# All transposes of the activation on VectorE, in squares of 32x32, in place of TensorE

## The reference: what must be computed

```python
gate = lora_add(einsum('bnh,fh->bnf', x, W_gate), x, A_gate, B_gate)   # 512 -> 1376
up   = lora_add(einsum('bnh,fh->bnf', x, W_up),   x, A_up,   B_up)
act  = silu(gate) * up
down = lora_add(einsum('bnf,hf->bnh', act, W_down), act, A_down, B_down) # 1376 -> 512
return x + down
# lora_add(base, inp, A, B) = base + (inp @ A[i].T) @ B[i].T * 0.5, i by batch
```

## Time and profile before

| | us |
|---|---|
| median of 3 runs | 559.76 (559.27 to 559.87) |
| the profiled execution | 559.44 |
| its span | 557.6 |
| TensorE busy | 519.3 (93%) |
| VectorE busy | 260.4 (47%) |
| ScalarE busy | 199.9 (36%) |
| GpSimd busy | 39.8 (7%) |

### The profile page before, as it was taken

One profiled execution on the slowest core, in us unless ns is written; L12 is line 12 of the kernel. 1 busy time (PEld: TensorE's weight loads), 2 busy tenths in 40 slices (PEclk: granted clock), 3 DMA queues, 4 the chain that ended last, 5 costly groups with the idle time before them and its releaser, 6 DMA issues.

```text
span 557.6 us, 10117 instructions
## 1 busy us (share of the span) xinstructions
PE 519.3 (93%) x3169; PEld 472.5 (85%) x3169; DVE 260.4 (47%) x558; ACT 199.9 (36%) x427; POOL 39.8 (7%) x55
## 2 busy tenths in 40 slices
PE   0098899999999999999999999999999999999997
PEld 0097787989898989999898989898989898999986
DVE  7894266544444435353435353534444443435341
ACT  4890008333333433243323233323333343324221
POOL 1015700100000000000000000000000000000000
PEclk9999899999999999999999999999999999999999
DMA  7799991312030404030303031211203040403000
GB/s 288 293 303 389 325 322 44 78 47 78 22 105 6 118 0 117 6 111 13 111 13 106 18 92 32 83 41 52 71 22 101 7 116 0 120 3 111 13 21 19
DMA packets 32306, 53.19 MB, mean 95 GB/s; under 512 B 7586, under 2 KB 16194, under 8 KB 32290
## 3 DMA queue, kind: packets, MB, share of 16 engines
q1 hardware_dynamic: 32290, 53.00, 31.0%
HBM read 48.69 MB, written 4.28 MB: 95 GB/s over the span
## 4 chain that ended last, share of the span: by engine, by line
PE 86%; DVE 6%; DMA 4%; ACT 1%; issue 1%; SPq 0%; DVEq 0%
PE ps_g L962 21%; PE ps_u L962 20%; PE ps_db L1000 13%; PE ps_da L1000 13%; PE ps_x L991 3%; PE ps_x L942 3%; PE ps_g L916 2%; DMA toep<-kpad 2%; PE ps_u L916 2%; PE ps_g L972 2%; PE ps_u L972 2%; PE ps_g L973 2%; PE ps_u L973 2%; DMA kpad<-k_sb 2%; PE ps_x L1034 1%
## 5 line engine op out<-in xcount | busy, mean ns | idle before, releaser
L470 ACT CAST b_spl<-b_raw 64x512 fp32r<-64x512 f32 (+1 forms) x96 | 54.4, 569 | 98.6 <-PE ps_u L973 79.5
L780 DVE TENSOR_TENSOR b_spl<-b_raw,b_spl 64x512 fp32r<-64x512 f32 (+1 forms) x96 | 60.4, 630 | 53.7 <-ACT b_spl L470 50.1
L962 PE MATMUL ps_g<-w_hi,x_hi 128*128 128x512 f32 (+1 forms) x192 | 72.7, 379 | 1.4 <-DVE x_lo L874 1.4
L962 PE MATMUL ps_u<-w_hi,x_hi 128*128 128x512 f32 (+1 forms) x192 | 71.4, 372 | 0.0
L962 PE MATMUL ps_u<-w_lo,x_hi 128*128 128x512 f32 (+1 forms) x192 | 71.3, 371 | 0.0
L962 PE MATMUL ps_u<-w_hi,x_lo 128*128 128x512 f32 (+1 forms) x192 | 71.3, 371 | 0.0
L962 PE MATMUL ps_g<-w_lo,x_hi 128*128 128x512 f32 (+1 forms) x192 | 71.1, 370 | 0.0
L962 PE MATMUL ps_g<-w_hi,x_lo 128*128 128x512 f32 (+1 forms) x192 | 71.0, 370 | 0.0
L816 DVE TENSOR_TENSOR h_act<-h_act,ps_u 128x512 f32<-128x512 f32 (+1 forms) x48 | 30.3, 632 | 54.3 <-PE ps_u L973 54.2
L1000 PE MATMUL ps_da<-wd_hi,ht_hi 128*128 128x288 f32 (+1 forms) x176 | 54.6, 310 | 0.0
L1000 PE MATMUL ps_db<-wd_hi,ht_hi 128*128 128x288 f32 (+1 forms) x176 | 53.3, 303 | 0.0
(11 more groups left out here) (169 smaller groups left out, 894.4 us busy)
## 6 DMA issues: line engine op xcount, KB each, us to landing
a_raw<-atab SPq DMA_DIRECT2D x64, 152.0 KB, 2.4
toep<-kpad SPq DMA_DIRECT2D x16, 512.0 KB, 6.8
b_raw<-btab SPq DMA_DIRECT2D x128, 64.0 KB, 2.1
um<-xr SPq DMA_DIRECT2D x16, 256.0 KB, 4.7
x<-xT SPq DMA_DIRECT2D x8, 512.0 KB, 7.9
w_raw<-wgu SPq DMA_DIRECT2D x8, 512.0 KB, 9.1
out<-y_sb SPq DMA_DIRECT2D x15, 256.0 KB, 2.1
b_raw<-btab SPq DMA_DIRECT2D x64, 44.0 KB, 1.8
```

The source lines that it names most:

```text
L470: nc.scalar.copy(b_spl[0:LR, up, 0:w], b_raw[slot][:, up * w:(up + 1) * w]).then_inc(b_hi, 1)
L780: V.tensor_tensor(b_spl[LR:P, up, 0:w], b_raw[slot][:, up * w:(up + 1) * w], b_spl[0:LR, up, 0:w].bitcast(F32), ALU.subtract).then_inc(b_l ...
L962: T.matmul(ps[:, 0:w], xs[:, q, kb, :], ws[:, kb, col:col + w], start=(kb == 0 and xs is x_hi and ws is w_hi), stop=False)
```

## The change

The blocks of 128x128 on TensorE are gone. `transpose_act` is now a function of VectorE. It is called with a chunk and with the quarters of the tokens that it is to do (`froms`). One instruction takes 32 tokens (partitions `tok * 32` on of `h_act`) and, of each block of 128 columns, the 32 that begin at `to * 32`; it transposes the 4 (in the last chunk 3 or 2) squares of 32x32 and writes them to partitions `to * 32` on of the bank. 16 instructions make a chunk. The calls are put between VectorE's other work: chunks 0 and 1 in two halves, chunk 2 in one piece. With it `gated(2)`, `b_lo_part(na, nq, 0, .)` and, on ScalarE, `ht_hi_part(1)` move. The waits of the old function move along, save the wait for `amaskt_ok`, which is VectorE's own earlier work. The last block of chunk 2 has 96 hidden rows; its `to` = 3 has two squares.

```diff
--- before.py
+++ after.py
@@ -24,6 +24,7 @@
 NM = 64
 NF = 1376
 FB = -(-NF // P)
+Q = 32
 FLAST = NF - (FB - 1) * P
 R = 16
 BT = 4
@@ -531,10 +532,10 @@
                     top_part(NP_GU + 5)
                 ht_hi_part(0)
                 silu(2)
+                ht_hi_part(1)
                 if not last:
                     b_hi_part(na, nq, 0, 0)
                     b_hi_part(na, nq, 0, 1)
-                ht_hi_part(1)
                 act.wait_ge(res_ps, t + 1)
                 wait(act, y_out, 16 * t)
                 nc.scalar.copy(y_sb[:, :], ps_x[0][:, :]).then_inc(res_ok, 1)
@@ -815,6 +816,28 @@
                     dve.wait_ge(u_ps, n + 1)
                     V.tensor_tensor(h_act[:, s, 0:w], h_act[:, s, 0:w], ps_u[s][:, 0:w], ALU.mult).then_inc(act_ok, 1)
 
+                def transpose_act(c, froms):
+
+                    nf, w = BLK[c][1], CH[c][1]
+                    s = (NC * q + c) % 2
+                    bank = [0, 1, 1][c]
+                    if froms[0] == 0:
+                        dve.wait_ge(act_ok, NC * t + c + 1)
+                        if c == 0:
+                            dve.wait_ge(tm_ok, t + 1)
+                        elif c == 1:
+                            wait(dve, tdlo_ok, t)
+                        else:
+                            dve.wait_ge(htlo_ok, (NC + 1) * t + 2)
+                    for tok in froms:
+                        for to in range(P // Q):
+                            n = len(range(to * Q, w, P))
+                            flat = h_act[tok * Q:(tok + 1) * Q, s, :].rearrange("t (f q) -> t f q", q=P)
+                            into = ps_x[bank][to * Q:(to + 1) * Q, :].rearrange("q (f t) -> q f t", t=P)
+                            ins = V.transpose(into[:, 0:n, tok * Q:(tok + 1) * Q], flat[:, 0:n, to * Q:(to + 1) * Q])
+                    if froms[-1] == P // Q - 1:
+                        ins.then_inc(ht_ps, 1)
+
                 def ht_lo_part(c):
                     f0, nf = BLK[c]
                     bank = [0, 1, 1][c]
@@ -837,6 +860,7 @@
                 b_lo_part(a, q, 1, 0)
                 gated(0)
                 b_lo_part(a, q, 1, 1)
+                transpose_act(0, (0, 1))
                 if not first:
                     finish(t - 1)
                 dve.wait_ge(bd_hi, t + 1)
@@ -845,21 +869,24 @@
                 if first:
                     rem_part(NP_GU + 2)
                     rem_part(NP_GU + 3)
+                transpose_act(0, (2, 3))
                 b_lo_part(a, q, 2, 0)
                 gated(1)
                 b_lo_part(a, q, 2, 1)
+                transpose_act(1, (0, 1))
                 if first:
                     rem_part(NP_GU + 4)
                     rem_part(NP_GU + 5)
                 ht_lo_part(0)
+                transpose_act(1, (2, 3))
+                gated(2)
                 if not last:
                     b_lo_part(na, nq, 0, 0)
-                gated(2)
-                if not last:
-                    b_lo_part(na, nq, 0, 1)
                 ht_lo_part(1)
+                transpose_act(2, (0, 1, 2, 3))
                 if not last:
                     x_lo_part(na, nq, False)
+                    b_lo_part(na, nq, 0, 1)
                 ht_lo_part(2)
                 dve.wait_ge(ad_ps, t + 1)
                 wait(dve, td_ps, t)
@@ -973,25 +1000,6 @@
                     T.matmul(ps[:, 0:w], t_lo[:, up, :], b_spl[:, up, 0:w], start=False,
                              stop=True).then_inc(u_ps if up else g_ps, 1)
 
-                def transpose_act(c):
-                    f0, nf = BLK[c]
-                    s = (NC * q + c) % 2
-                    bank = [0, 1, 1][c]
-                    pe.wait_ge(act_ok, NC * t + c + 1)
-                    if c == 0:
-                        pe.wait_ge(tm_ok, t + 1)
-                    elif c == 1:
-                        wait(pe, tdlo_ok, t)
-                        if first:
-                            pe.wait_ge(amaskt_ok, 1)
-                    else:
-                        pe.wait_ge(htlo_ok, (NC + 1) * t + 2)
-                    for f in range(nf):
-                        rows = P if f0 + f < FB - 1 else FLAST
-                        ins = T.transpose(ps_x[bank][0:rows, f * P:(f + 1) * P], h_act[:, s, f * P:f * P + rows],
-                                          ident[:, :])
-                    ins.then_inc(ht_ps, 1)
-
                 def down(f, bank):
 
                     rows = P if f < FB - 1 else FLAST
@@ -1023,11 +1031,9 @@
                 for up in range(2):
                     base(1, up)
                     lora(1, up)
-                transpose_act(0)
                 for up in range(2):
                     base(2, up)
                     lora(2, up)
-                transpose_act(1)
 
                 pe.wait_ge(htlo_ok, (NC + 1) * t + 1)
                 for kb in range(KB):
@@ -1038,7 +1044,6 @@
                     pe.wait_ge(w_rem_dve, len(pieces) - NP_POOL)
                 pe.wait_ge(ad_lo, t + 1)
                 down_chunk(0)
-                transpose_act(2)
                 pe.wait_ge(htlo_ok, (NC + 1) * t + 2)
                 down_chunk(1)
                 if not last:
```

## The result

| | before | after |
|---|---|---|
| median of 4 runs, us | 559.76 | 669.22 (668.14 to 670.18) |
| ratio to before | | 1.195, 95% interval 1.193 to 1.198 |
| span of the profiled execution, us | 557.6 | 667.4 |
| VectorE / TensorE busy | 47% / 93% | 75% / 81% |
| one middle tile, us | 29.4 | 36.0 |

What follows compares the result with a forecast made beforehand. TensorE bounds the kernel before, VectorE's loop after: 12.1 (first tile) + 14 x 6.3 + 5.0 (last) = 105.3 us more, span 557.6 to 663, so 665 us; own range 635 to 700, overall 590 to 710.

Steps and rivals of the forecast that it cites:

- What bounds, and the turn-over: TensorE bounds before, 29.42 us per tile; after, the loop over VectorE does, 35.7 us, 6.3 more per tile.
- The transposes, 16.1 us per tile: On VectorE, 48 added transposes per tile: 32 at 0.35 us, 12 at 0.317 and 4 at 0.283.
- a square's filling: In each VectorE transpose, 32 columns' time added for filling one square: 0.03 us.
- Held apart: On VectorE, successive transposes write other partitions, so they start 0.32 us apart before filling, like `t_lo`, not 0.21.
- The loop without the squares, 9.43 + 10.2: Per tile, 9.43 us from last `down` blocks to next `gated(0)`, then 10.2 us of VectorE's old instructions and ScalarE detour.
- The waits: TensorE idles 7.5 us per tile: some 0.4 for `b_lo(2,0)`, then 2.2, 1.8 and 3.0 for the three `ht_lo`.
- First tile: Last `down` blocks start at 122.0 instead of 109.91, 12.1 us later; VectorE also splits weights there.
- The last tile: From `gated(0)` to the last blocks 24.3 us instead of 19.24, 5.0 us more.
- Rival 3: On TensorE, the granted clock falls in its new waits; chance 0.11.
- Rivals 1, 2 and 4: 1: overlap, 545 us, 0.03; 2: not held apart, 592 or 566, 0.12; 4: other rate, 759 or 619, 0.05/0.03.

Runs made afterwards that it cites:

- dose runs: The changed kernel with half or a quarter of the transposes left out, two PSUM fills added: 551.95 us (24 per tile) and 594.85 us (36 per tile).
- the exchanged loops: The changed kernel with the two inner loops, over `tok` and `to`, exchanged, so the output's place stays and the input's changes: 670.16 us.
- the filler run: The changed kernel with matmuls nobody reads put ahead of TensorE's waits for `ht_lo(1)` (4) and `ht_lo(2)` (9): 656.21 us, ratio 1.173.
- the copies: The changed kernel with a plain copy in place of each transpose, same places and sizes: 640.58 us, ratio 1.144.

## Why the prediction was right, and where it was not

- **What bounds, and the turn-over: right.** TensorE was the bound; the loop that runs over VectorE from `gated(0)` to `ht_lo(2)` became it. The dose runs show both sides of the knee.
- **The transposes, 16.1 us per tile: mis-sized by 0.7.** Measured 15.4. The spacing of 128 columns was 0.333 us, not 0.35: the gap after a held transpose is 0.01 us where I took the 0.04 of `t_lo`. The 0.03 us for a square's filling were my estimate, and no run shows a filling; what the runs show in its place is a transpose that lasts 33 ns longer than a copy of the same places.
- **Held apart: right, its reason too narrow.** I gave the output's place alone; the exchanged loops show that the input's counts as well. Had I relied on that reason to propose a better loop order, I would have been wrong by some 45 us.
- **The loop without the squares, 9.43 + 10.2: right.** 15.4 added gives 35.0; the filler run has 35.15.
- **The waits: right in place**, and each of the three for `ht_lo` 0.2 us shorter than forecast, once the idle-before is read as said above.
- **First tile: right but for the squares.** Its last `down` blocks start at 121.29, forecast 122.0; 11.4 us later than before, not 12.1. The last tile takes 23.65 us from `gated(0)` to its last blocks, 4.4 more than before, not 5.0.
- **Rival 3, the clock: it came, beside the forecast and not in its place.** I gave it 0.11, with a fall in every tile. The one fall of before has a mean clock of 0.66 over 5 us, and 0.50 in the stretch from 61 to 64 us; that makes, as an estimate, 3.4 us at half speed and up to 1.7 us lost per fall. In the kernel after a fall cost 1.5 us in every second tile: behind the first, behind 7 of the 14 middle ones and behind the last, 14 us in all.
- **That the number is within 4 us is luck.** At full clock the steps add up to 11.4 + 14 x (25.71 + 9.45 - 29.42) + 4.4 = 96 us, where I had 105: 9 us too much, nearly all of it the squares. The clock's 14 us were left out. 96 + 14 = 110 is what the span grew by (667.4 - 557.6), and two errors of opposite sign left 665 for a measured 669.
- **Rivals 1, 2 and 4: excluded** by the spacing of 0.333 us, and for the faster rate by the copies (0.92 ns a column).

## What to carry to other kernels

Work moved to an engine that is half idle fits only in the gaps that end before the next reader's deadline: follow the loop between the two engines step by step (here 9.4 + 10.2 us against TensorE's 28.2 left room for 8.6 us at most, and 24 transposes of 7.7 us, standing where they did, already cost 0.4), and move as much as fits there. Sixteen of the 48 transposes gave 1.0% and all of them cost 19.5%. Count small instructions by their spacing under the conditions that they will have, which for VectorE here included whether the next one read or wrote other partitions (it then started 0.00 to 0.02 us after the end of the one before, and otherwise 0.08 to 0.09 us before it). And put down for a new wait on TensorE not only its length but what the granted clock may do behind it (here 1.5 us behind 7 of the 14 middle tiles).

## What the runs showed of the hardware

- A transpose of 32 partitions from SBUF to PSUM in float32 lasts 0.323, 0.287 and 0.264 us for 128, 96 and 64 columns, 33 ns more than a copy of the same places. The four blocks of a chunk take VectorE 16 x 0.333 = 5.3 us; TensorE does them in 0.44.
- VectorE held the next transpose back to the end of the one before (0.00 to 0.02 us after it) when the partitions of its input or of its output changed; where neither did, it started 0.08 to 0.09 us before that end.
- With waits of 1.8, 1.5 and 2.5 us in each tile the granted clock fell behind 7 of the 14 middle tiles and stayed at 1.00 behind the others; such a fall cost 1.5 us. Why it comes in one tile and not in the next is not shown. Here the level changes 0.6 us after TensorE has gone on at 336.81 (granted clock 1.00 from there to 337.40, 0.51 from 337.40 to 340.20), and the distance of the matmuls' starts goes from 0.13 to 0.24 us (kernel after, TensorE in order of time):

```profile
337.18 0.29 PE L1008 MATMUL ps_db<-wd_hi,ht_lo 128*128 128x288 f32 x1
337.31 0.29 PE L1008 MATMUL ps_db<-wd_hi,ht_hi 128*128 128x288 f32 x1
337.44 0.39 PE L1008 MATMUL ps_db<-wd_lo,ht_hi 128*128 128x288 f32 x1
337.63 0.44 PE L1008 MATMUL ps_db<-wd_hi,ht_lo 128*128 128x288 f32 x1
...
338.12 0.44 PE L1008 MATMUL ps_db<-wd_lo,ht_hi 96*128 96x288 f32 x1
338.36 0.44 PE L1008 MATMUL ps_db<-wd_hi,ht_lo 96*128 96x288 f32 x1
```

Matmuls that nobody reads, put into the two later waits, kept the clock at 1.00 behind each of the first 15 tiles and won 13 us back.
